# Attention on one core: the values of a key tile in two halves of 256 query columns, one behind each half of the scores

## The reference

```python
q, k, v = (x @ Wq.T), (x @ Wk.T), (x @ Wv.T)          # split into 16 heads of 32
attn = softmax(einsum('nhqd,nhkd->nhqk', q, k) / sqrt(32))
x = layernorm(x + einsum('nhql,nhld->nhqd', attn, v))
w = (weights >= 0) * 2 - 1
x = layernorm(x + clip((x @ w.T) * scale + bias, -100, 100))
```

## Time and profile before

| | before |
|---|---|
| median of the runs | 2724.6 us (2723.04, 2724.60, 2725.27) |
| span of the profiled execution | 2721.4 us; the profile gives no other time of its own for it, so the runs' median stands 3.2 us above it |
| PE, DVE, ACT, POOL busy | 2686.9, 2308.4, 2261.1, 341.1 us |
| exponential, 2048 | 1877.7 us |
| score matmuls, 16384 records | 1117.4 us |
| value matmuls, 8192 records | 1060.5 us |

### The profile page before, as it was taken

How to read it: one execution, slowest core, us unless ns; L and a number is a source line. 1 busy time by engine, 2 the same in 40 slices (tenths; PEclk the granted TensorE clock), 3 DMA queues, 4 the chain that set the end, 5 groups by cost and what they waited for, 6 DMA issues and landing times.

```text
span 2721.4 us, 76294 instructions
## 1 busy us (share of the span) xinstructions
PE 2686.9 (99%) x32088; PEld 1351.0 (50%) x32088; DVE 2308.4 (85%) x1983; ACT 2261.1 (83%) x2726; POOL 341.1 (13%) x342
## 2 busy tenths in 40 slices
PE   9999999999999999999999999999999999979998
PEld 8888888733333333333333333333333333337887
DVE  7444444389999999999999999999999999978998
ACT  5333333399999999999999999999999999965665
POOL 1000000000000000010000000000000000005665
PEclk9999999999999999999999999999999999989999
DMA  6555555557686777768677686867768677655553
GB/s 227 191 194 193 188 186 186 197 132 169 132 176 140 155 157 158 162 126 184 138 153 165 142 172 135 167 147 157 168 131 172 141 159 158 150 145 177 189 189 136
DMA packets 216706, 445.22 MB, mean 164 GB/s; under 512 B 15570, under 2 KB 130258, under 8 KB 189780
## 3 DMA queue, kind: packets, MB, share of 16 engines
q0 software_dynamic: 27504, 200.29, 37.4%
q1 hardware_dynamic: 179108, 222.61, 26.2%
q10 hardware_dynamic: 9792, 17.83, 1.7%
HBM read 122.43 MB, written 117.96 MB: 88 GB/s over the span
## 4 chain that ended last, share of the span: by engine, by line
ACT 48%; PE 31%; issue 16%; DMA 3%; DVE 2%; SPq 0%; DVEq 0%; POOL 0%; ACTq 0%; POOLq 0%
ACT probs L769 48%; PE banks L226 19%; PE banks L1007 7%; DMA total<-partial 2%; PE banks L632 1%; PE banks L996 1%; PE banks L661 1%; PE banks L989 1%; PE banks L1003 1%; DVE partial L818 1%; DVE total L821 0%; DVE partial L821 0%; PE banks L248 0%; PE banks L990 0%; PE banks L254 0%
## 5 line engine op out<-in xcount | busy, mean ns | idle before, releaser
L769 ACT ACTIVATE probs<-banks 128x1024 f32<-128x1024 f32 x2048 | 1877.7, 1457 | 3.9 <-PE banks L632 3.9
L632 PE MATMUL banks<-score_rows 97*32 97x512 f16 x16384 | 1117.4, 380 | 4.5 <-issue 4.0
L661 PE MATMUL banks<-probs,v_keys 128*32 128x512 f32 x8192 | 1060.5, 592 | 0.1
L821 DVE TENSOR_TENSOR partial<-partial,probs 128x2048 f32<-128x2048 f32 x384 | 879.4, 2290 | 33.4
L632 PEld LDWEIGHTS banks<-score_rows 97*32 97x32 f16 x16384 | 361.3, 95 | 708.2 <-ACT probs L769 484.3
L818 DVE TENSOR_TENSOR partial<-probs 128x2048 f32<-128x2048 f32 x192 | 439.6, 2290 | 23.6 <-ACT probs L769 16.7
L601 POOL DMA_DIRECT2D total<-partial x191 | 164.7, 862 | 1713.7 <-DMA total<-partial 703.3
L661 PEld LDWEIGHTS banks<-probs,v_keys 128*32 128x32 f32 x8192 | 249.0, 111 | 209.9 <-ACT probs L769 0.2
L821 DVE TENSOR_TENSOR total<-total,probs 128x2048 f32<-128x2048 f32 x128 | 292.6, 2286 | 6.8
L354 DVE TENSOR_TENSOR qk_lo<-banks,qk_hi 128x512 f16<-128x512 f32 x128 | 88.3, 690 | 241.6 <-ACT qk_hi L309 241.6
L680 PEld LDWEIGHTS banks<-total,ones 128*32 128x32 f32 x3584 | 105.6, 109 | 280.7 <-issue 265.1
(11 more groups left out here) (95 smaller groups left out, 2117.5 us busy)
## 6 DMA issues: line engine op xcount, KB each, us to landing
total<-partial POOLq DMA_DIRECT2D x191, 1024.0 KB, 8.3
scratch_q_raw<-qk_raw SPq DMA_DIRECT2D x16, 1024.0 KB, 5.7
scratch_k_raw<-qk_raw SPq DMA_DIRECT2D x16, 1024.0 KB, 5.7
scratch_v<-v_out SPq DMA_DIRECT2D x16, 1024.0 KB, 5.1
score_rows<-scratch_q_hi SPq DMA_DIRECT2D x128, 128.0 KB, 4.6
score_rows<-scratch_k_hi SPq DMA_DIRECT2D x128, 128.0 KB, 3.5
v_keys<-scratch_v SPq DMA_DIRECT2D x64, 256.0 KB, 5.8
scratch_attn<-wf_scaled SPq DMA_DIRECT2D x64, 256.0 KB
```

The costliest lines, as they stand in the source:

```text
L632: last = nc.tensor.matmul(scores_of(phase, unit)[part, i, :], k_rows[:, h, keys], q_rows[:, h, qb * BLK:(qb + 1) * BLK], start=True, stop= ...
L661: last = nc.tensor.matmul(banks[rows, out_bank(qb), :], v_keys[:, kt, rows], probs[:, kt % P_RING, h, :], start=(kt == 0), stop=(kt == KT ...
L769: nc.scalar.activation(probs[:, kt % P_RING, heads, :], scores_of(it % SLOTS, qb * UNITS + u), ACT.Exp, scale=SCALE / GAIN ** 2).then_inc( ...
L821: nc.vector.tensor_tensor(into, into, probs[:, kt % P_RING], ALU.add).then_inc(a_sum, 1)
```

## The change

The value matmuls take 256 of the 512 query columns at a time. Part 0 stands behind the first score unit of the tile two ahead, part 1 behind the second. Part 0 does all the waits that the values had, part 1 increments `a_pv`. Only part 0 of a block's first tile carries the start flag. The score functions get the half as an argument, and their waits for q and k stay with half 0.

```diff
-        def fast_scores(it, phase, qb, kt):
-            if kt == 0:
+        def fast_scores(it, phase, qb, kt, halves=(0, 1)):
+            if kt == 0 and halves[0] == 0:
                 pe.wait_ge(a_q[qb], it * FIRST_Q + FIRST_Q)
...
-            for half in range(2):
+            for half in halves:
                 unit = qb * UNITS + 2 * kt + half
...
-        def values(it, qb, kt):
+        def values(it, qb, kt, part):
+
             st = it * QB + qb
...
+            cols = slice(part * BLK // 2, (part + 1) * BLK // 2)
+            if part == 0:
+                if qb == 0 and kt % TPB == 0:
+                    pe.wait_ge(a_v[kt // TPB], it * 16 + 16)
+                pe.wait_ge(a_prob, st * UNITS + 2 * kt + 2 + SLOTS)
+                if kt == 0:
+                    pe.wait_ge(a_dout, st + 1)
             for h in range(G):
                 rows = slice(HD * h, HD * h + HD)
-                last = nc.tensor.matmul(banks[rows, out_bank(qb), :], v_keys[:, kt, rows], probs[:, kt % P_RING, h, :],
-                                        start=(kt == 0), stop=(kt == KT - 1))
-            last.then_inc(a_pv, 1)
+                last = nc.tensor.matmul(banks[rows, out_bank(qb), cols], v_keys[:, kt, rows], probs[:, kt % P_RING, h, cols],
+                                        start=(kt == 0 and part == 0), stop=(kt == KT - 1), skip_group_check=True)
+            if part == 1:
+                last.then_inc(a_pv, 1)
...
             for kt in tiles:
-                if kt + LAG < KT:
-                    scores(it, phase, qb, kt + LAG)
...
-                values(it, qb, kt)
+                for half in range(2):
+                    if kt + LAG < KT:
+                        scores(it, phase, qb, kt + LAG, (half,))
...
+                    values(it, qb, kt, half)
```

More of the change, by code:

```diff
@@ L616, in _ @@
         pe.sem_inc(a_merged, GROUPS - 1)
-        def fast_scores(it, phase, qb, kt):
-            if kt == 0:
+        def fast_scores(it, phase, qb, kt, halves=(0, 1)):
+            if kt == 0 and halves[0] == 0:
                 pe.wait_ge(a_q[qb], it * FIRST_Q + FIRST_Q)
-            if qb == 0 and kt % TPB == 0:
+            if qb == 0 and kt % TPB == 0 and halves[0] == 0:
                 pe.wait_ge(a_k[kt // TPB], it * FIRST_K + FIRST_K)
-            for half in range(2):
+            for half in halves:
                 unit = qb * UNITS + 2 * kt + half
@@ L634, in fast_scores, with exact_scores @@
                 last.then_inc(a_score, 1)
-        def exact_scores(it, phase, qb, kt):
+        def exact_scores(it, phase, qb, kt, halves=(0, 1)):
             st = it * QB + qb
-            if kt == 0:
+            if kt == 0 and halves[0] == 0:
                 pe.wait_ge(m_q, st * 32 + 32)
-            if kt % TPB == 0:
+            if kt % TPB == 0 and halves[0] == 0:
                 pe.wait_ge(m_k[kt // TPB % 2], (st * QB // 2 + kt // TPB // 2) * 16 + 16)
             keys = slice(kt % (2 * TPB) * P, (kt % (2 * TPB) + 1) * P)
-            for half in range(2):
+            for half in halves:
                 unit = qb * UNITS + 2 * kt + half
@@ L686, in steps @@
             for kt in tiles:
-                if kt + LAG < KT:
-                    scores(it, phase, qb, kt + LAG)
[L689 to L692, removed]
-                values(it, qb, kt)
+                for half in range(2):
+                    if kt + LAG < KT:
+                        scores(it, phase, qb, kt + LAG, (half,))
+                    elif qb < QB - 1:
+                        scores(it, phase, qb + 1, kt + LAG - KT, (half,))
+                    elif it is not LAST:
+                        scores(it + 1, phase + 1, 0, kt + LAG - KT, (half,))
+                    values(it, qb, kt, half)
                 if kt in DEN_TILES and qb > 0:
```

## The result

The changed kernel takes 2742.3 us (median of four runs, 2739.1 to 2742.7), the one before in the same comparison 2723.8. The ratio is 1.0064, 95% interval [1.0051, 1.0076]: 18.4 us slower. The forecast was no change, 2721 to 2730 us, with 0.11 on slower. It failed, and not by the mechanism that it had as its first rival.

A forecast was written before the change was run, and what follows sets the result against it. ACT's exponential was taken to bound the kernel; ACT's chain 0, stage end +0.01 us, PE's 0.32 us a block hidden: span 2721.4 us unchanged, plus 3.2 us, gives 2724.6 us, range 2721 to 2730 us.

The forecast's parts named there:

- its first rival: PE's entry from scores into values and back: seams make PE the bound, 31 us slower, 2755 us, chance 0.06.
- The bound: Attention stage: ACT's exponentials run end to end, 0.917 us apart; PE has 0.04 us to spare in a tile.
- Columns, loads, seams: PE's tile: columns 0.01 us, weight loads 0, seams 0.01; together +0.02 us (bounds 0 and 0.25), hidden.
- Rivals 1 and 2: On PE: two new seams a tile, 2755 us, chance 0.06; value weight loads lying bare, 2929 us, chance 0.03.
- The moved score half: First score half on PE comes 0.39 us earlier: worth 0 now, thickens ACT's cushion of ready scores.
- Code: PE's instruction stream: 8192 more matmuls and loads; instruction fetch takes 0.6% of the DMA engines, cost 0.
- nobody is near: Second values half behind a score-slot wait: its users, an exponential 8 tiles later and DVE's output copy, aren't close.
- Rival 3: Behind the seventh denominator piece: ACT starves for a moment in each block, 6 us, 2731 us, chance 0.04.
- the signs of being wrong: Exponentials of about 1.02 us behind gaps ending at scores, 256-column round pairs well over 0.45 us, or PE idle at issue.

The follow-up runs named there:

- quarters: Changed kernel with the order of before and the values in four parts of 128 columns, whole merges: 3060.1 us, ratio 1.1257.
- e1: Changed kernel with the order of before: both score units first, then both halves of the values: 2743.0 us, ratio 1.0064.
- g2: Order of before, values in four parts of 128 columns, merges of one head of four (denominators incomplete): 2726.3 us, ratio 1.0009.
- g3: Kernel before with its whole values placed between the two score units, no record added: 2726.6 us, ratio 1.0009.
- f4: Changed kernel's order and halves in even tiles only, order and whole values of before in odd ones: 2732.2 us, ratio 1.0028.
- e3: Changed kernel with merges of the partial sums moving one head of four (256 KB, not 1 MB; denominators incomplete): 2722.9 us, ratio 0.9995.

## Why the prediction was wrong

**The bound, right.** ACT runs end to end, and PE has a little to spare. Nothing in any run with the narrow scores speaks against it: where code comes in time, the changed kernel and even the quarters run at ACT's pace.

**Columns, loads, seams, right and on the safe side.** I gave PE's tile +0.02 us. Behind a stop, where PE runs as fast as it can, a score unit and its half of the values take 1390.25 to 1391.12 = 0.87 us, so 1.74 us a tile, no more than the 1.75 read before. The values by themselves show the price: where nothing holds PE up, a tile's values take 0.861 us with 4 matmuls (before), 0.865 with 8 (e1) and 0.875 with 16 (g2). I had put 0.01 for the columns; it is 0.004. Rivals 1 and 2 were priced at 31 and 205 us and are false: the quarters with small merges have four times the value matmuls and stay within 3 us.

The rule that the prediction cites from the Trainium skill, "TensorE: Matmul & The Clock Gate", Part 3 (The mechanism), that a weight load overlaps matmuls in flight only where its row group differs, isn't borne out here: 32 loads of 110 ns in a tile in place of 8 cost 0.014 us together. The same section names a second case, a load into the background weight buffer, which the prediction left out; these times fit that one.

**The moved score half, right.** 0.39 us of cushion were forecast and 1857 - 1470 ns measured, in the run where nothing else disturbs (1857 - 1492 = 365 ns against the kernel before with the same small merges).

**Code, the step that failed.** It stood in one sentence: 8192 matmuls and loads more, "instruction fetch takes 0.6% of the DMA engines now, cost 0". The share was right (0.7% after) and was the wrong quantity; the runs put about 11 of the 18.4 us there. Code isn't a matter of bandwidth but of a deadline: 16384 bytes must be there before PE has used up the 256 instructions before them. In every run here the transfer of a block starts after PE has entered the one before, or some 2 us ahead of that at most, and PE never goes on into it sooner than 2.2 us behind the start of the transfer. So a block is late when its transfer starts less than 2.2 to 2.9 us before the one before is used up.

The traces of the stage (560 to 2420 us) give both sides. "Late start" is a transfer that starts over 2.4 us after PE has entered the block before; how long a block lasts is taken where no stop lies at its end:

| kernel | records in a plain tile | a block lasts, us: shortest, median | late starts | stops at block distances |
|---|---|---|---|---|
| before | 48 | 7.2, 8.5 | 68 of 219 | 0 |
| order alone (g3) | 48 | 7.0, 8.6 | 65 of 218 | 0 |
| every second tile (f4) | 56 | 6.1, 7.5 | 114 of 249 | 4 |
| changed | 64 | 5.7, 6.5 | 129 of 280 | 29 |
| changed, small merges (e3) | 64 | 5.7, 6.5 | 6 of 282 | 0 |
| quarters (f1) | 96 | 4.0, 4.5 | 138 of 348 | 132 |
| quarters, small merges (g2) | 96 | 4.0, 4.5 | 13 of 408 | 14 |

The 9.8 and 7.3 us above hold for plain tiles only. A denominator piece adds 16 records to its tile, so a block lasts 7.2 to 10.1 us before and 5.7 to 7.3 us in the changed kernel where nothing stops it (e3). The kernel before was no safe place either: a third of its transfers start late, the latest 5.9 us after PE has entered a block, and its tightest block was entered 2.5 us behind the start of its transfer, 0.3 us from the least that any run shows. The Trainium skill has the mechanism ("Runtime: NRT & Kernel Launch", Instruction fetch mechanics): blocks of 256 instructions, the next one fetched while the current one runs, the cost mostly hidden. The block size agrees with the trace. "Mostly hidden" holds for 48 records a tile, fails a little at 64 and badly at 96, and nearly holds again at 96 once the merges are small (3 us and 14 stops).

**The merge, not thought of.** This is the second step that failed: I had written that nobody is near who waits for what PE's new order moves, and had given the wait at the first denominator piece no term. But the last merge of a block lands only just before PE asks for it. The order alone (g3) makes PE wait 4.4 us there in place of 0.5. It brings PE to a piece 0.43 us after the start of the last score unit, where before it was 1.29 and in the changed kernel it is 0.87. The cut alone (e1) keeps the 1.29 and makes PE wait 8.2 us, both together 9.1. Why longer code in the old order lengthens the wait at the merge isn't settled: the merges' own time to landing moved little (median 8.3 us before, 8.6 in both). The 2.8 us by which the span grew behind the last exponential lie here too: the last store of denominators is issued at 2455.68, 13.0 us after the last exponential starts, and was at 2436.27, 10.0 us after. PE starts on the last block's pieces 2.0 us later behind that exponential, once the merge has landed, and they take 1.0 us longer, at a granted clock of 0.50 (2451 to 2455.5 us) against 0.71 (2432 to 2436.5) before.

**The range and the chances.** Rival 3, ACT starving for a moment in each block, described the shape of the loss (gaps at the scores behind lone stops) but had its place and its cause wrong, and got 0.04. Of the signs of being wrong, two came true: exponentials of 1.02 us behind gaps that end at the scores, and idle time on PE put down to issue. The prediction tied the first to its rivals and the second to no cause.

## What to carry to other kernels

When a change adds instructions to an engine whose program is laid out in full, divide 256 by the new rate of instructions, in the densest stretch and not in the plain one, and compare this with how late a code transfer can be while the DMA engines are full (up to 6 us, and 2.2 to 2.9 until PE goes on, in these runs), not the bytes with the bandwidth. A cut into smaller instructions on an engine that isn't the bound can then slow the engine that is. Less DMA traffic beside it took the loss away here; whether the same bytes in smaller or spread-out DMAs would do so wasn't run. And where an engine has little to spare, look up each wait that it passes without stopping: a transfer that lands just in time is as near as the bound.

## What the runs showed that was not expected

- Code blocks come late in steps, not in proportion: 0 stops at block distances with 48 records in a plain tile, 4 with 56, 29 with 64, and 132 with 96, where PE's waits for "issue" are 198 us at scores and values alone.
- Code transfers start later beside bulk DMAs: the median start is 2.2 us after PE has entered the block before in the changed kernel, and 0.5 us with merges of 256 KB in place of 1 MB.
- 0.12 us for a change between 128-wide and 32-wide matmuls, none for a change between fp16 scores and fp32 values at the same width, and rounds of 128 columns (0.107 us) with four loads of 110 ns each cost a tile's values 0.014 us in all.
- Semaphore increments on PE between matmuls aren't free even where PE has queued work: 16 of them cost 0.9 us.
- A stop of PE of 2.3 us was followed by a stretch with part of it at the lower clock in e1 (granted clock 0.79 over 8 us), while the one of 2.4 us at 1390 us in the changed kernel was not (granted clock 1.00 in both windows around it).
